# The landmark softmax of a Nyström attention in groups of two batches, with another order of the work around it

## The reference

```
q_l, k_l = landmark means of q and k            # 128 landmarks, 91 of them distinct here
attn1 = softmax(q   @ k_l.T)                    # tokens x landmarks
attn2 = softmax(q_l @ k_l.T)                    # landmarks x landmarks, one per batch and head
attn3 = softmax(q_l @ k.T)                      # landmarks x tokens
z = attn2.T / (max row sum * max column sum)    # both maxima over ALL batches and heads
6 times: az = attn2 @ z
         z = 0.25 * z @ (13 I - az @ (15 I - az @ (7 I - az)))
out = (attn1 @ z) @ (attn3 @ v) + convolution(v)
```

## Time and profile before

| | |
|---|---|
| runs shown, us | 755.29, 757.77, 2143.39; median 757.77 |
| the profiled execution | 756.43 us, of which the span is 754.4 us |
| granted clock of PE, mean | 0.926 |
| busy, share of the span | PE 91%, PEld 70%, DVE 58%, ACT 46%, POOL 31% |
| the costliest group of PE | L676, 768 matmuls from ST 91.6 us and 768 from NN 89.3 us |
| the opening stage | 51.9 us to 106.6 us, where the first matmul of L676 begins |

### The profile page before, as it was taken

One profiled execution on the slowest core, in us unless ns is written; L12 is line 12 of the kernel. 1 busy time (PEld: TensorE's weight loads), 2 busy tenths in 40 slices (PEclk: granted clock), 3 DMA queues, 4 the chain that ended last, 5 costly groups with the idle time before them and its releaser, 6 DMA issues. The chain is left out here.

```text
span 754.4 us, 14900 instructions
## 1 busy us (share of the span) xinstructions
PE 683.4 (91%) x6016; PEld 528.6 (70%) x6016; DVE 437.3 (58%) x863; ACT 345.5 (46%) x774; POOL 237.0 (31%) x211
## 2 busy tenths in 40 slices
PE   8689688999999989898979999969999999998896
PEld 4488577888798879798867555547666666657565
DVE  3405848686868585958545333325777777764422
ACT  4425443544535445353326555514555555544531
POOL 6433433434454443534431022103222222201001
PEclk9758779999999999999986999975999999997999
DMA  8100000000000000000000000000000000000000
GB/s 321 50 0 2 1 2 2 1 2 1 2 3 2 1 2 2 1 2 2 1 2 0 1 2 0 1 1 1 2 1 1 1 1 1 1 1 1 1 14 17
DMA packets 4988, 8.47 MB, mean 11 GB/s; under 512 B 3576, under 2 KB 4088, under 8 KB 4536
## 3 DMA queue, kind: packets, MB, share of 16 engines
q1 hardware_dynamic: 4328, 7.46, 2.8%
q10 hardware_dynamic: 592, 0.07, 0.1%
HBM read 6.97 MB, written 0.55 MB: 10 GB/s over the span
## 5 line engine op out<-in xcount | busy, mean ns | idle before, releaser
L944 POOL TENSOR_TENSOR STD<-STD,NN 91x492 f32<-91x492 f32 (+1 forms) x96 | 104.0, 1100 | 152.2 <-DVE NN L1082 94.1
L676 PE MATMUL PS<-ST 128*91 128x123 f32 x768 | 91.6, 271 | 6.0 <-DVE ST L1088 5.9
L676 PE MATMUL PS<-NN 128*91 128x123 f32 (+1 forms) x768 | 89.3, 267 | 8.6 <-DVE NN L1082 8.5
L676 PEld LDWEIGHTS PS<-NN 128*91 128x91 f32 x768 | 81.3, 159 | 16.8 <-DVE NN L1082 13.0
L676 PEld LDWEIGHTS PS<-ST 128*91 128x91 f32 x768 | 83.3, 159 | 11.3 <-DVE ST L1088 8.3
L1082 DVE SCALAR_TENSOR_TENSOR NN<-ST,PS 91x492 f32<-91x492 f32 x96 | 62.3, 660 | 49.1 <-PE PS L676 49.1
L1704 PE MATMUL PS<-QR,KA 128*128 128x270 f32 x256 | 72.5, 414 | 0.0
L1818 DVE TENSOR_SCALAR CL<-PS,K 128x270 f32<-128x270 f32 x144 | 65.6, 495 | 9.9 <-PE PS L1704 4.5
L864 ACT ACTIVATE STD<-ST 91x492 f32<-91x492 f32 (+1 forms) x96 | 51.4, 561 | 41.0 <-DVE ST L1088 40.9
L1088 DVE SCALAR_TENSOR_TENSOR ST<-PS,STD 91x492 f32<-91x492 f32 (+1 forms) x96 | 55.3, 598 | 11.7 <-PE PS L676 8.6
L1759 ACT ACTIVATE EX<-CL,NG 128x540 f32<-128x540 f32 x64 | 46.7, 741 | 32.8 <-DVE CL L1818 32.8
(11 more groups left out here) (325 smaller groups left out, 1253.0 us busy)
## 6 DMA issues: line engine op xcount, KB each, us to landing
MB<-mat SPq DMA_DIRECT2D x1, 2048.0 KB, 9.3
TP<-taps SPq DMA_DIRECT2D x1, 1204.0 KB, 16.1
MA<-mat SPq DMA_DIRECT2D x1, 1120.0 KB, 11.3
WI<-wide SPq DMA_DIRECT2D x1, 902.0 KB, 13.0
CO<-const SPq DMA_DIRECT2D x1, 512.0 KB, 13.8
out<-OS SPq DMA_DIRECT2D x8, 45.0 KB
XA<-xpatch SPq DMA_DIRECT2D x1, 256.0 KB, 2.9
CO<-const SPq DMA_DIRECT2D x1, 192.0 KB
```

The lines of the kernel that those rows point to most:

```text
L676: last = nc.tensor.matmul(PS[0:NL, PINV + q, h % 4 * SW + c0:(h % 4 + 1) * SW], x[:, h, 0:NL], x[:, h, c0:SW], start=True, stop=True)
L944: nc.gpsimd.tensor_tensor(TD[:, 4 * q:4 * q + 4, c0:SW], SA[:, 4 * q:4 * q + 4, c0:SW], NN[0:NL, 4 * q:4 * q + 4, c0:SW], ALU.subtract).th ...
```

## The change

Scores are made for two batches at a time: `scores(p)` writes 16 matrices to the same four banks, four to a bank, and `shifted`, `halved` and `summed` work on the pair, in tiles of twice the size. What `halved` did at its end is now `other_half`. `normalised` and `sums` still go batch by batch. The loops and the tables `ALONG` are replaced by written orders. In them batch 0's `project` and `values` come between the first two pairs, `scores3` before the fourth, `turn3` before `scores1` (and from f_e3, no more behind f_sub1), `scores1` after the last scores, now in banks 0 to 3. `start(0)` stands before `sums(6)`. On ACT `exps1(0)` comes last before `opened(0)`; on DVE `top1`, `shift1` and `small` come after the last `summed`. POOL clears its five tiles in one go before the first `normalised`.

```
--- before
+++ after
@@ -532,11 +532,11 @@
 UU = ts("UU", [128, 2, H, DH])
 OC = ts("OC", [128, 2, N])
 QL = STD[:, :].rearrange("p (s j b n) -> p s j b n", s=3, j=4, b=2)
-DD = ts("DD", [NL, 2, 2, NL])
-EE = ts("EE", [NL, 2, H, NL])
-MX = ts("MX", [NL, 2, 4])
-ZZ = ts("ZZ", [NL, 2, 3, H])
-ZR = ts("ZR", [NL, 2, H])
+DD = ts("DD", [NL, 2, 4, NL])
+EE = ts("EE", [NL, 2, 2 * H, NL])
+MX = ts("MX", [NL, 4, 4])
+ZZ = ts("ZZ", [NL, 2, 3, 2 * H])
+ZR = ts("ZR", [NL, 2, 2 * H])
@@ -603,18 +603,25 @@
         last.then_inc(sem("f_s3"), 1)

     def scores1(b):
-        pe.wait_ge(sem("f_e3"), upto(b, 1, 1))
+        if b:
+            pe.wait_ge(sem("f_e3"), upto(b, 1, 1))
+        else:
+            pe.wait_ge(sem("n_sub"), BP)
+            pe.wait_ge(sem("n_half"), BP)
         for hh in range(2):
             for t in range(2):
                 for r in range(4):
                     rows = slice(32 * r, 32 * r + 32)
                     c = (2 * hh + t) * NL
-                    last = nc.tensor.matmul(PS[0:UT, bank(b, r), c:c + NL], QM[rows, hh, t * UT:(t + 1) * UT],
+                    last = nc.tensor.matmul(PS[0:UT, r, c:c + NL], QM[rows, hh, t * UT:(t + 1) * UT],
...
     def turn3(b, t):
-        pe.wait_ge(sem("f_sub1"), upto(b, 2, 2))
+        if b:
+            pe.wait_ge(sem("f_sub1"), upto(b, 2, 2))
+        else:
+            pe.wait_ge(sem("f_e3"), 1)
@@ -736,16 +743,17 @@
                                         XAP[:, p, U:UL], start=True, stop=True)
         last.then_inc(sem("n_proj"), 1)

-    def scores(i):
-        pe.wait_ge(sem("n_qk"), 2 * (i // 2) + 2)
-        if i:
-            pe.wait_ge(sem("n_sub"), i)
-            pe.wait_ge(sem("n_half"), i)
-        for h in range(H):
-            r, hh = h % 4, h // 4
-            rows = slice(32 * r, 32 * r + 32)
-            last = nc.tensor.matmul(PS[0:KP, SCORES + r, hh * KP:(hh + 1) * KP], QL[rows, i // 2 % 3, hh, i % 2, :],
-                                    QL[rows, i // 2 % 3, 2 + hh, i % 2, :], start=True, stop=True)
+    def scores(p):
+        pe.wait_ge(sem("n_qk"), 2 * p + 2)
+        if p:
+            pe.wait_ge(sem("n_sub"), p)
+            pe.wait_ge(sem("n_half"), p)
+        for g in range(4):
+            o, hh = divmod(g, 2)
+            for r in range(4):
+                rows = slice(32 * r, 32 * r + 32)
+                last = nc.tensor.matmul(PS[0:KP, SCORES + r, g * KP:(g + 1) * KP], QL[rows, p % 3, hh, o, :],
+                                        QL[rows, p % 3, 2 + hh, o, :], start=True, stop=True)
         last.then_inc(sem("n_score"), 1)

     def sums(i):
@@ -758,34 +766,40 @@
                                     start=c == 0, stop=c == B * H - 1, skip_group_check=True)
         last.then_inc(sem("n_sums"), 1)

-    def turn3_both(b):
-        turn3(b, 0)
-        turn3(b, 1)
-
-    ALONG = {0: project, 1: values, 3: scores3, 5: scores1, 7: turn3_both}
     proj(0, 0)
     proj(0, 1)
+    scores(0)
+    proj(1, 0)
+    project(0)
+    proj(1, 1)
+    values(0)
+    proj(2, 0)
+    scores(1)
+    proj(2, 1)
+    proj(3, 0)
+    scores(2)
+    proj(3, 1)
     pe.wait_ge(sem("n_slide"), 2)
-    for i in range(B):
-        scores(i)
-        if i + 1 < B // 2:
-            proj(i + 1, 0)
-        if i >= 2:
-            sums(i - 2)
-        if i in ALONG:
-            ALONG[i](0)
-        if i + 1 < B // 2:
-            proj(i + 1, 1)
-    sums(B - 2)
-    sums(B - 1)
+    sums(0)
+    sums(1)
+    scores3(0)
+    scores(3)
+    sums(2)
+    sums(3)
+    turn3(0, 0)
+    turn3(0, 1)
+    scores1(0)
+    sums(4)
+    sums(5)
     weigh(0)
+    turn_weighed(0)
+    start(0)
+    sums(6)
+    sums(7)
     pe.wait_ge(sem("n_diag"), 1)
     pe.wait_ge(sem("n_ones"), 1)
-    pe.wait_ge(sem("n_sub"), B)
-    pe.wait_ge(sem("n_half"), B)
+    pe.wait_ge(sem("f_sub1"), 2)
     nc.tensor.matmul(PS[0:NL, TOPS, 0:DH], ON[:, :], CG[:, :], start=True, stop=True).then_inc(sem("n_tops"), 1)
-    turn_weighed(0)
-    start(0)
     for b in range(B):
         body(b)
@@ -880,42 +894,54 @@
...
         if part:
             nc.scalar.copy(dst, src).then_inc(sem("n_qk"), 1)
         else:
             nc.scalar.mul(dst, src, SC).then_inc(sem("n_qk"), 1)

-    def halved(i):
-
-        act.wait_ge(sem("n_max"), i + 1)
-        if i >= 2:
-            act.wait_ge(sem("n_a"), i - 1)
-        for h in (0, 1, 4, 5):
-            r, hh = h % 4, h // 4
-            last = nc.scalar.activation(EE[:, i % 2, h, :], PS[0:NL, SCORES + r, hh * KP:hh * KP + NL], ACT.Exp,
-                                        bias=MX[:, hh, r:r + 1], accum_out=ZZ[:, i % 2, 0, h:h + 1])
+    def halved(p):
+
+        act.wait_ge(sem("n_max"), p + 1)
+        if p >= 2:
+            act.wait_ge(sem("n_a"), 2 * p - 2)
+        for r in range(2):
+            for g in range(4):
+                h = 4 * g + r
+                last = nc.scalar.activation(EE[:, p % 2, h, :], PS[0:NL, SCORES + r, g * KP:g * KP + NL], ACT.Exp,
+                                            bias=MX[:, r, g:g + 1], accum_out=ZZ[:, p % 2, 0, h:h + 1])
         last.then_inc(sem("n_half"), 1)
-        act.wait_ge(sem("n_sub"), i + 1)
-        nc.scalar.activation(EE[:, i % 2, :, :].rearrange("p (k r) n -> p k r n", k=2)[:, :, 2:4, :],
+
+    def other_half(p):
+
+        act.wait_ge(sem("n_sub"), p + 1)
+        nc.scalar.activation(EE[:, p % 2, :, :].rearrange("p (g r) n -> p r g n", r=4)[:, 2:4, :, :],
                              DD[:, :, :, :], ACT.Exp).then_inc(sem("n_exp"), 1)

-    ALONG = {0: query, 4: exps3, 6: exps1, 7: turned3}
     warm(ACT.Exp)
     copied(0, 0)
     copied(0, 1)
-    for i in range(B):
-        if i + 1 < B // 2:
-            copied(i + 1, 0)
-        halved(i)
-        if i == 7:
-            act.wait_ge(sem("n_pad"), PADS)
-        if i in ALONG:
-            ALONG[i](0)
-        if i + 1 < B // 2:
-            copied(i + 1, 1)
+    copied(1, 0)
+    query(0)
+    copied(1, 1)
+    halved(0)
+    copied(2, 0)
+    other_half(0)
+    copied(2, 1)
+    halved(1)
+    copied(3, 0)
+    other_half(1)
+    copied(3, 1)
+    halved(2)
+    other_half(2)
+    exps3(0)
+    halved(3)
+    other_half(3)
+    act.wait_ge(sem("n_pad"), PADS)
+    turned3(0)
     weighed(0)
+    exps1(0)
     act.wait_ge(sem("n_rck"), 1)
     opened(0)
@@ -947,10 +973,11 @@
                 normal1(b + 1)

     def normalised(i):
-        pool.wait_ge(sem("n_zr"), i + 1)
-        pool.wait_ge(sem("n_e0"), i + 1)
-        nc.gpsimd.tensor_tensor(AA[0:NL, i, :, 0:NL], EE[:, i % 2, :, :],
-                                ZR[:, i % 2, :].unsqueeze(2).broadcast_to([NL, H, NL]),
+        p, own = i // 2, slice(i % 2 * H, (i % 2 + 1) * H)
+        pool.wait_ge(sem("n_zr"), p + 1)
+        pool.wait_ge(sem("n_e0"), p + 1)
@@ -962,14 +989,11 @@
     nc.gpsimd.tensor_copy(SL[:, DH - 1:DH], CO[0:NL, C_DV:C_DV + 1]).then_inc(sem("n_slide"), 1)
     nc.gpsimd.memset(ON[:, :], 1.0).then_inc(sem("n_ones"), 1)
     pads = [P3[D:128, :, :, :], ST[D:128, :, :, :], NN[D:128, :, :], PT[D:128, :, :, :], UU[D:128, :, :, :]]
+    pool.wait_ge(sem("n_slide"), 2)
+    for k, pad in enumerate(pads):
+        nc.gpsimd.memset(pad, 0.0).then_inc(sem("n_pad"), 1)
+        pool.wait_ge(sem("n_pad"), k + 2)
     for i in range(B):
-        if i < PADS - 1:
-            if i:
-                pool.wait_ge(sem("n_a"), i)
-            else:
-                pool.wait_ge(sem("n_slide"), 2)
-            nc.gpsimd.memset(pads[i], 0.0).then_inc(sem("n_pad"), 1)
-            pool.wait_ge(sem("n_pad"), i + 2)
         normalised(i)
     normal1(0)
@@ -998,7 +1022,7 @@
                         ).then_inc(sem("f_m3"), 1)

     def halves1(b):
@@ -1096,25 +1120,23 @@
                     for work in FRONT.get(k, ()):
                         work(b + 1)

-    score = PS[0:NL, SCORES:SCORES + 4, 0:2 * KP].rearrange("p r (k n) -> p r k n", k=2)[:, :, :, 0:NL]
+    score = PS[0:NL, SCORES:SCORES + 4, 0:4 * KP].rearrange("p r (g n) -> p r g n", g=4)[:, :, :, 0:NL]

     def shifted(i):
         dve.wait_ge(sem("n_score"), i + 1)
-        v.tensor_reduce(MX[:, :, :].rearrange("p k r -> p r k"), score, AX.X, ALU.max, negate=True
-                        ).then_inc(sem("n_max"), 1)
+        v.tensor_reduce(MX[:, :, :], score, AX.X, ALU.max, negate=True).then_inc(sem("n_max"), 1)
         dve.wait_ge(sem("n_max"), i + 1)
         if i:
             dve.wait_ge(sem("n_exp"), i)
-        v.tensor_tensor(DD[:, :, :, :].rearrange("p k r n -> p r k n"), score[:, 2:4, :, :],
-                        MX[:, :, 2:4].rearrange("p k r -> p r k").unsqueeze(3).broadcast_to([NL, 2, 2, NL]),
-                        ALU.add).then_inc(sem("n_sub"), 1)
...
         e = EE[:, i % 2, :, :]
         z = ZZ[:, i % 2, :, :]
...
-                        e.rearrange("p (k r) n -> p k r n", k=2)[:, :, 2:4, :], AX.X, ALU.add
+        v.tensor_reduce(z[:, 0, :].rearrange("p (g r) -> p g r", r=4)[:, :, 2:4],
...
```

(59 more changed lines are left out.)

## The result

The changed kernel is **slower**: 764.85 us median (757.96 to 768.42) against 758.79 for the kernel before, 16 runs each; the ratio is 1.009, 95% interval 1.0063 to 1.0117. That is within 2%, as the chances had it, but 10 us above the 754.9 forecast and above the range's end of 759.5. The profiled execution took 760.1 us, span 757.9, and lies at the fast end; a second one of the same kernel (e5) took 765.95, span 763.7.

The account below looks back on a forecast made before the run. The opening stage was taken as a chain of hand-overs, no engine full, drawn out by a half clock. RCK at 103.6 instead of 105.09 gives 1.5 us: 756.43 - 1.5 = 754.9 us, range 750.5 to 759.5.

Parts of the forecast that it names:

- I let the clock fall at 83 and return at 93: Opening stage: half clock from PE's idle time before sums(2), at 83 us, until 93.
- the chain: Opening stage: hand-overs walked one after another from `project` to RCK, reached at 104.3 us, 103.6 after a correction.
- the 0.7 allowed for overlap: End of the opening stage: half the chained old order's error (106.5, not 105.09) taken off, RCK 104.3 to 103.6.
- the pause before sums(2): PE in the opening stage: nothing to do between 79.7 and 83.3, 3.6 us idle.
- a rival, which shares its 0.2 with another: Clock falls already at 73, before scores(2), returns at 80: RCK 105.8, 757.1 us; chance 0.2 with a later return.
- The return at 80: Opening stage, rival case: the clock, fallen at 73, is full again at 80; RCK 105.8, 757.1 us.
- The rival "slower": Opening stage: clock at half from 83 until RCK, RCK at 108.7, 3.6 us lost, 760.0 us; chance 0.13.
- The 4.7 us: ACT, old order: last landmark batch's first exp spent 4.7 us behind batch 0's `exps1`; the change takes this out.
- Behind RCK the order stays: Loop behind the opening stage: same order, `total1`, `normal1`, then `turn1`, for which PE waits 1.52 us.
- The level: Starting time of the kernel before: the profiled execution's 756.43 us, 1.3 below the median of the runs shown.
- POOL's clearings: Five clearings ahead of POOL's first product in the opening stage: price 0, over by 62 us.
- the prediction's rule against the change: Transposes count less as PE activity than matmuls, so `turn3` in the slow stretch keeps the clock down longer; no size.

Follow-up runs that it names:

- e5: The changed kernel again, unedited, for a second trace: 765.8 us median, ratio 1.011 to the kernel before.
- e4: The changed kernel with `turn_weighed(0)` and `start(0)` behind the sums and L802's matmul again, `small(0)` behind L1178: 762.9 us, ratio 1.007 to the kernel before.
- e8: The changed kernel with `summed(1)` ahead of `top3(0)` on DVE: 760.3 us, ratio 1.005 to the kernel before.
- e10: The changed kernel with `summed(1)` ahead of `top3(0)` and `sums(6)`, `sums(7)` ahead of `start(0)`, no extra matmuls: 755.2 us, ratio 0.994 to the kernel before.
- e2: The kernel before with extra, unread matmuls before sums(2), sums(3), sums(5), turn3 and turn1(0): 758.6 us, ratio 1.002 to the kernel before.
- e3: The kernel before with batch 0's `exps1` on ACT moved behind `weighed(0)`: 753.3 us, ratio 0.997 to the kernel before.
- e1: The changed kernel with extra, unread matmuls where PE waited, from scores(1) to turn1(0): 758.9 us, ratio 1.002 to the kernel before.
- e7: The changed kernel with only the last ten extra matmuls of e1, from behind sums(7) to turn1(0): 761.2 us, ratio 1.004 to the kernel before.
- e9: The order of e10 with the extra matmuls of e1, less those whose pause is gone: 749.2 us, ratio 0.990 to the kernel before.

## Why the prediction was wrong

**The step that failed is the clock's.** "I let the clock fall at 83 and return at 93" was measured as 67 to 94 and as 69 to 103. Everything else in the chain up to RCK held. If I walk the same chain with the first trace's clock, moved by its earlier start of 1.5 us, it gives about 107.4, less the 0.7 allowed for overlap 106.7; measured on that base was 105.35 + 1.5 = 106.9. The prices of single operations were right: scores of a pair 0.93 at full and 1.61 at half (1.0 and 1.7 foreseen), maxima 1.67 (1.66), DD 0.91 (0.87), exp of DD 0.84 (0.8), a pair's exps 2.5 (2.5). The place of `exps3`, the pause before sums(2) (3.6 foreseen, 3.2 found), `top3` with DVE idle ahead of it and `start` ahead of the sums came as described.

**Why I got the clock wrong.** I looked for one long pause, the 3.6 us before sums(2), and let the clock fall there. It fell 15 us earlier, behind the 1.47 us ahead of scores(1). The chain puts those scores at 67.7, and PE's work ahead of them ended at 66.9 in my walk; I gave that pause no price. The next pause, from 71.6 to 73.0 ahead of scores(2), I used only for a rival, which shares its 0.2 with another. In both traces of the changed kernel the clock was at half before it; it is the pause behind which e4 and e8 fell. The return at 80 did not come. The rival "slower" (half from 83 to RCK, 760.0) was right in sign and was given 0.13; its decisive point, the clock at `start(0)`, was wrong, as the clock was full there (1.93 us) in both traces and the stage had lost its time by then.

**What is the clock worth here?** Over the executions of one kernel, span goes with time at half clock: pooled over 221 executions of 12 kernels (two outliers of the kernel before, at 862 and 3498 us, left out), 0.36 us of span to 1 us at half, the slope taken within each kernel (0.26 to 0.53 for single kernels). Between the kernels, before has 113.9 us at half and a mean span of 754.8 (85 executions), after, with e5, 129.6 and 762.5 (22): 15.7 x 0.36 = 5.7 of the 7.7 us. For e10 against after the same sum gives (129.6 - 112.0) x 0.36 = 6.3 of 10.0 us (762.5 - 752.5). So by this estimate about three quarters of the change's loss, and under two thirds of what the reordering gave back, come with the clock; the remainder is not divided further. It is a division by correlation, over executions on different chips: e2 warns that it is not what an added matmul buys, and e8 and e10 removed pauses and chain length together.

**The 4.7 us** of waiting behind `exps1` were read as the gain to be had. e3 shows 1.7 us of it on the path. The rest was covered by `turn3` behind L1012 and by sums(6) behind `turn3`.

**"Behind RCK the order stays"** was true of the order and not of the time: 1.6 and 1.7 us were lost there in the two traces, where PE's pause before `turn1` is longer (2.24, from 1.52) and the clock at half behind it. But a longer pause is not what it takes: every trace of the new order but e1's has this fall, also those with the pause filled to 1.1 (e7, e9) or at 1.51 (e4), and none of the old order's four has it. Which part of the new order brings it is open. I had written that this pause swallows the earlier `opened(0)`. It did, and by that it grew: PE reached the wait earlier and stood longer. The blocks behind RCK were also to stay within 1 us; together they moved by 3.2 in the first trace, half of it in the rest, which moves as much from trace to trace.

**The level.** The 16 runs of before have a median of 758.8, not the 756.4 that I took from two runs and a profiled one. That is 2.4 of the 10 us of miss. The other 7.6 are the 1.5 us of gain that did not come and the 6.1 us of loss (758.8 to 764.9) that did.

**POOL's clearings** cost nothing, as foreseen: over at 60.6, with the first product at 70.7. **DVE's small instruction beside POOL**, once L1031, cost what was said, 1.36 us; it was off the path in the first trace.

**Open:** what grouping in pairs is worth by itself. No run has the new order without the groups, since the groups force `scores3` and the projections into other places. Nor is it shown why the pause ahead of scores(1) ends in a fall in the traces of after, e5, e7 and e10 and not in those of e4 and e8.

## What to carry to other kernels

Where the granted clock falls behind pauses of PE, price an order by its pauses on PE as well as by its chain: walk the chain once with the clock at half from the first pause, and if the result changes sign, give that case a chance like the forecast's own. Compare medians, not traces: two traces of one kernel differed by 5.8 us of span (757.9 and 763.7), and the change cost 6.1. When a wait is removed, name what the same engine's neighbours wait for at that time before booking it as gain (4.7 us seen, 1.7 had). And in orders written by hand, look at every instruction that waits with ready work behind it; two such swaps on DVE and PE were worth about 1.4% here.

## What the runs showed of the hardware

- A busy PE did not bring the clock back. From 73 to 83 in the first trace after, PE was busy for 8.91 of 10 us and stayed at half; from 72.45 to 81.90 it had no pause at all:

```profile
73.00:83.00 10.00, 8.91 (x87) 8.23 (x86) 4.39 (x5) 4.66 (x23) 0.47 (x1) 0.50 0.00 1
72.45:81.90 9.45, 9.45 (x91) 8.78 (x88) 3.79 (x3) 3.72 (x18) 1.02 (x1) 0.50 0.00 1
```

  In e5 it was busy for 29.60 of 34 us. In e1 the clock came back at 77.8, 3.8 us after PE's last pause and in the same code. The Trainium skill (TensorE: Matmul & The Clock Gate, Part 4: PE-mode transpose) says that transposes do not count as a busy PE in the way matmuls do. There is none between 73 and 83, and e5's 34 us hold 2.70 us of them, so they cannot explain it. By the prediction's rule against the change `turn3` keeps the clock down for longer: in the first trace after, the clock had been at half for 23 us when `turn3` began at 90.13, and came back at 94.1, 1.3 us after it; whether it delayed the return is not shown.
- DVE instructions with two operands in on-chip memory are held up by POOL as well, not only TENSOR_SCALAR. After `summed(2)` in the trace after, beside two products of POOL (87.79 to 90.55, 1.38 us each):

```profile
88.33 0.88 DVE L1045 SCALAR_TENSOR_TENSOR Z<-Z 91x8 f32<-91x8 f32 x1
89.24 1.32 DVE L1048 SCALAR_TENSOR_TENSOR Z<-E,Z 91x8 f32<-91x8 f32 x1
92.29 1.36 DVE L1055 TENSOR_SCALAR Z<-Z,CO 91x8 f32<-91x8 f32 x1
```

  The first two do 8 elements each and end with POOL's first and second product; in e10's trace they took 0.88 and 1.33, again beside POOL. In the trace before they took 0.16 each, with POOL idle:

```profile
94.16 0.16 DVE L1021 SCALAR_TENSOR_TENSOR Z<-Z 91x8 f32<-91x8 f32 x1
94.35 0.16 DVE L1024 SCALAR_TENSOR_TENSOR Z<-E,Z 91x8 f32<-91x8 f32 x1
```

  They add about 1.9 us to DVE between `summed(2)` and `summed(3)`. In the trace after, ACT's exps of the last pair end at 89.9 and `summed(3)` starts at 90.5, 0.6 us late; the path did not feel it, as POOL's last product was done at 95.0 and the sums that need it ran at 100.75. What POOL does matters too. Beside its clearing of PT in the trace before (76.69, 1.99 us) TENSOR_SCALAR was held up (0.12 at 66.89, with POOL idle) and SCALAR_TENSOR_TENSOR, with two such operands, was not:

```profile
77.55 0.16 DVE L1120 SCALAR_TENSOR_TENSOR ZZ<-EE,ZZ 91x8 f32<-91x8 f32 x1
...
77.87 0.84 DVE L1124 TENSOR_SCALAR EE<-EE 91x8 f32<-91x8 f32 x1
```
